# First attention: the value products of a job's four row blocks in one step

## The reference, cut to what matters

```
QEr  = einsum('bhsd,ld->bhsl', q, Er);  Srel = _skew(QEr)
QK   = einsum('bhsd,bhtd->bhst', q, k)
attn = softmax(where(causal, (QK + Srel) / sqrt(16), -inf))
out  = einsum('bhst,bhtd->bhsd', attn, v)
```

## Time and profile before

| | |
|---|---|
| median of 3 runs | 2192.8 us (2190.79 to 2193.58) |
| profiled execution | 2194.78 us |
| its span, from the first to the last instruction | 2193.1 us |
| TensorE matmul busy | 1909.3 us, 87% |
| VectorE, ScalarE, GpSimd busy | 1013.6, 854.2, 604.6 us |
| chain that ended last, by engine | PE 79%, POOL 6%, issue 5%, DVE 5%, ACT 3%, DMA 1% |
| chain, line L692 (the value products) | 2% |

### The profile page before, as it was taken

The page is one execution under the profiler, slowest core; times in us unless marked ns, Lnnn a source line. Parts: engine busy times, 40 slices in busy tenths (PEclk is TensorE's granted clock), DMA queues, the critical chain, the costliest instruction groups (busy, mean ns, idle before and its releaser), DMA issues.

```text
span 2193.1 us, 32078 instructions
## 1 busy us (share of the span) xinstructions
PE 1909.3 (87%) x10730; PEld 1108.3 (51%) x10731; DVE 1013.6 (46%) x2762; ACT 854.2 (39%) x2087; POOL 604.6 (28%) x543
## 2 busy tenths in 40 slices
PE   4899999599999963999999089999999999967998
PEld 2355555254344452666676034445445445446886
DVE  3366667634554243222222444444444444445775
ACT  2477777324444420333333044444444444421000
POOL 0011111301111115000000656665655555631000
PEclk8799999699999765999999589999999999986999
DMA  3677776300000352011100500000000000020001
GB/s 135 216 262 268 267 264 232 116 0 1 1 1 1 117 194 82 29 33 33 33 31 24 206 1 1 1 1 1 1 1 1 1 1 1 1 77 1 0 0 38
DMA packets 63567, 146.59 MB, mean 67 GB/s; under 512 B 6280, under 2 KB 41232, under 8 KB 58832
## 3 DMA queue, kind: packets, MB, share of 16 engines
q1 hardware_dynamic: 60368, 136.55, 18.1%
q0 software_dynamic: 3072, 8.39, 1.1%
HBM read 86.21 MB, written 58.72 MB: 66 GB/s over the span
## 4 chain that ended last, share of the span: by engine, by line
PE 79%; POOL 6%; issue 5%; DVE 5%; ACT 3%; DMA 1%; SPq 0%; DVEq 0%; ACTq 0%; POOLq 0%
PE PS L598 13%; PE PS L1038 8%; PE PS L889 6%; PE PS L877 6%; PE PS L967 5%; PE PS L977 5%; PE PS L990 5%; PE PS L659 4%; PE PS L746 4%; PE PS L681 3%; POOL P L581 3%; PE PS L946 3%; PE PS L955 3%; PE PS L758 2%; PE PS L692 2%
## 5 line engine op out<-in xcount | busy, mean ns | idle before, releaser
L581 POOL TENSOR_SCALAR P<-P,rc 128x512 f32<-128x512 f32 x256 | 396.8, 1562 | 266.2 <-DVE rc L1568 266.2
L1222 ACT ACTIVATE P<-PS,nm 128x512 f32<-128x512 f32 x256 | 173.5, 682 | 320.0 <-DVE nm L1562 320.0
L1562 DVE TENSOR_REDUCE nm<-PS 128x2 f32<-128x1024 f32 x128 | 156.7, 1224 | 152.9 <-PE PS L967 152.9
L977 PEld LDWEIGHTS PS<-idf,P 128*128 128x128 f32 x1024 | 110.2, 141 | 135.1 <-POOL P L581 111.6
L977 PE MATMUL PS<-idf,P 128*128 128x128 f32 x1024 | 140.7, 281 | 35.5 <-POOL P L581 35.5
L1386 DVE CUSTOM_DVE_ANT_0 dump<-PS,maskw 128x128 f32<-128x128 f32 (+3 forms) x256 | 115.6, 488 | 116.0 <-PE PS L746 114.3
L1326 DVE CUSTOM_DVE_ANT_0 SN<-PS,SR 128x128 f32<-128x128 f32 (+3 forms) x256 | 115.3, 488 | 109.2 <-PE PS L663 108.8
L1150 ACT ACTIVATE PTf<-PS 128x512 f32<-128x512 f32 (+3 forms) x256 | 101.0, 439 | 151.5 <-PE PS L758 151.4
L877 PE MATMUL PS<-EW,hT 128*128 x640 | 146.6, 383 | 2.4 <-ACT hT L1197 2.4
L889 PE MATMUL PS<-EW,xT 128*128 x320 | 146.6, 601 | 1.8 <-ACT xT L1185 1.3
L967 PE MATMUL PS<-K,Q 64*128 64x512 f32 x512 | 144.6, 641 | 0.9 <-DVE Q L1550 0.9
(11 more groups left out here) (221 smaller groups left out, 3260.5 us busy)
## 6 DMA issues: line engine op xcount, KB each, us to landing
rel<-EN SPq DMA_DIRECT2D x16, 1024.0 KB, 4.8
SR<-rel SPq DMA_DIRECT2D x16, 1024.0 KB, 7.1
rel<-EN SPq DMA_DIRECT2D x16, 768.0 KB, 4.2
SR<-rel SPq DMA_DIRECT2D x16, 768.0 KB, 6.3
rel<-EN SPq DMA_DIRECT2D x16, 512.0 KB, 2.9
SR<-rel SPq DMA_DIRECT2D x16, 512.0 KB, 4.3
EW<-in_fc1T SPq DMA_DIRECT2D x8, 1024.0 KB, 11.8
EW<-in_fc2T SPq DMA_DIRECT2D x8, 1024.0 KB, 12.3
```

The costliest lines, as they stand in the source:

```text
L581: last = nc.gpsimd.tensor_scalar(P1[s % 4][:, j, :], P1[s % 4][:, j, :], rc1[:, s % 4, j:j + 1], None, ALU.mult)
L977: last = nc.tensor.transpose(TR1[j][:, c * P:c * P + P], P1[s % 4][:, j, c * P:c * P + P], idf[:])
L1222: last = af(P1[s % 4][:, j, :], PD[s % 2][:, j, :], ACT.Exp, bias=nm1[:, s % 4, j:j + 1], accum_out=sm1[:, s % 4, j:j + 1])
```

## The change

The value products of all four row blocks of a job are issued in step 4, in the order of the row blocks; before, row block u - 3 was issued in steps 3 to 6. Nothing else is edited.

```
-                    if n >= 1 and 3 <= u < 3 + RT:
-                        values_a(n - 1, u - 3)
+                    if n >= 1 and u == 4:
+                        for r in range(RT):
+                            values_a(n - 1, r)
```

## The result

The changed kernel takes 2202.6 us (median of 6 runs, 2198.6 to 2205.2), the kernel before 2193.0 (6 runs of the same sessions, 2190.8 to 2195.5): a ratio of 1.0040, with a 95% interval of 1.0028 to 1.0052. It is slower by 9.6 us, and the forecast was 2201.3.

A forecast was written before the change was run, and what follows sets the result against it. TensorE looked the bound, but ScalarE's score copy and VectorE's output stood close behind. Terms 7.0 + 0.8 + 1.0 gave 8.8, taken as 8.5 on 2192.8: 2201.3 us, range 2198 to 2203, wider 2195.5 to 2206.

The forecast's parts named there:

- The block: Step 4: all 80 value records in one group take 2.32 us; four groups were 2.68, saving 0.36 per job.
- Step 3 for nothing: Removing step 3's 8 value records gains nothing: its scores to step 4's stay 1.41 us, waiting for ScalarE's copy.
- EN late in steps 5 and 6: Without products, ScalarE's score copy is late: 1.84 us from step 5 scores to step 6, 2.27 from step 6 to 7.
- S7 to T0, ScalarE's queue: Step 7 scores to the next job's first scores: ScalarE's queue without slack makes the latter start 0.48 us late.
- its 5.43: Time in us from step 6 scores to the transposes after the next job's first scores, read from job 0.
- the projection is 0.58 late: Next job's key projection waits for VectorE's last output: 0.58 us late per job, 7.0 over jobs 1 to 12.
- Job 13 to job 14's transposes: At the end of job 13, transposes after the next first scores wait for VectorE's copies: 0.78 us late.
- Jobs 14 and 15: Jobs without relative scores: step 6 scores come 1.03 us late, the transposes that follow 0.49 late in each job.
- The range: 0.40 to 0.65 us a job giving 5.5 to 10 in all; kernel 2198 to 2203 us, widened to 2195.5 to 2206.
- A, TensorE bounds: Faster: score copies keep up, each job gains 0.36 us and the 0.58 gap goes; 2180 us, half of it 2187; 5%.
- B, the gap takes the delay up: No change: the 0.58 us gap before the next job's first scores absorbs the delay; 2194 to 2196 us; 13%.
- C, nothing is made up: Clearly slower: none of step 4's 1.76 us is made up, late scores reaching VectorE's maxima and loads; 2216 us; 3%.

The follow-up runs named there:

- block 0 put behind: Changed kernel with row block 0's 8 value records moved from step 4 to step 5, behind its transposes: job 20.21 us, median 2202.8 us, ratio to before 1.0041.
- early output copy: Changed kernel with ScalarE's output copy moved from step 6 to step 5, ahead of its relative-score copy: job 20.43 us, median 2202.8 us, ratio to before 1.0044.
- the kernel of 19.22 us a job: Kernel before, with block 3's products ahead of step 6's transposes and one VectorE probability copy moved to ScalarE: 2188.5 us, ratio 0.9960.
- later projections: Three projections and their copies one step later: on the changed kernel 2200.0 us; on the kernel before with block 3 ahead of step 6's transposes 2197.4 us.

## Why the prediction was right

- *The block.* 2.32 us was worked out from groups of 16 and 32; it stands 2.31 from its start to the next scores (211.89 to 214.20).
- *Step 3 for nothing.* S3 to S4 is 1.41 still. Shown by the profile after and, alone, by block 0 in step 4.
- *EN late in steps 5 and 6.* 1.84 and 2.26 against 1.84 and 2.27. Shown to be lack of cover by block 0 put behind, which used the idle for nothing.
- *S7 to T0, ScalarE's queue.* 2.67, as worked out. But the early output copy shows that this wait alone does not set the time. In the changed kernel the transposes behind T0 start 5.43 us after S6 with no idle ahead of them; with T0 0.34 earlier they start at 5.43 again, now after 0.34 of idle for VectorE's copy. ScalarE and VectorE allow them at the same moment. The prediction had both engines, with its 5.43 and its 0.58.
- *The term that was mis-sized* is the last: "the projection is 0.58 late", and "I see nothing that makes up the 0.58". The projection starts 0.59 late by the rows (12.02 after S4 in place of 11.43). But from its start to S1 it took 1.91 in place of 1.82, so a job pays 0.68, which is above the prediction's own 0.40 to 0.65 a job. The longer projection goes with its wait for VectorE's output. Wherever its first weight load waits for that output (0.09 to 0.17 us), in the kernel of 19.22 us a job too, the projection takes 1.91 to 1.92. Where it does not wait it takes 1.81: in job 0 of the same traces, in all steady jobs of the kernel before, and with later projections (226.34 to 228.15). The difference stands between the first and the second of its records. The trace of the kernel before had this case once, at the end of job 13, where it could have been read:

```profile
357.08 1.98 PE L598 MATMUL PS<-CTA,WAk 128*128 128x512 f32 x4
358.99 0.49 PE L663 MATMUL PS<-Ka,QPa 32*128 32x128 f32 x4
```

  Why a projection that waited takes 0.10 longer stays open. Twelve jobs make 8.0 in place of 7.0 (S4 of job 1 to S4 of job 13: 235.19 before, 243.23 after); 12 x 0.68 is 8.2, and the 0.17 less is the one long job (19.92) in the trace of the kernel before.
- *The rest of the sum.* Job 13 to job 14's transposes: 0.76, forecast 0.78. Jobs 14 and 15: 0.30 and 0.31, forecast 0.49 each. In job 14 S6 came 1.02 late, as forecast (1.03), but the next transposes started 5.25 after S6 (374.79 to 380.04) and not the 5.43 taken from job 0. In all it is 9.42 against 8.8, of which I had taken 8.5; the medians say 9.6. So the twelve jobs cost 1.0 more than forecast and the last ones 0.4 less, and it is partly luck that the sum came this close.
- *The range.* The prediction says that 0.40 to 0.65 a job give 5.5 to 10. With its 1.8 for the last jobs they give 6.6 to 9.6. The medians' 9.6 has an interval of about 6 to 11 us, so it bears out the size of the sum, and only the rows tell its terms.
- *Rivals.* A, TensorE bounds: excluded by each experiment that merged groups and got a longer job (block 0 to step 4, block 3 to step 5). Its counter-argument that in job 0 steps without products gain at most half of them was a little off: S6 to S7 gains 0.61 of 1.00. B, the gap takes the delay up: the gap did shrink from 0.58 to 0.28, but ScalarE and VectorE kept the rest. C, nothing is made up: of the block's 1.75, 0.38 and 0.62 were won back in steps 5 and 6 and 0.29 before T0. The loads and their masks play no visible part: TensorE's waits name none, and the kernels with blocks elsewhere follow the sums without them.

The rule of the Trainium skill that rotating banks cover an evacuation (Perfetto Trace Analysis, Matmuls) agrees: the relative scores don't rotate, and the price is 0.33 us of idle in each step without products. The drain at a change of tiling mode (TensorEngine Tiling (Array Packing), Key Properties) is consistent with 0.12 us a group, but no run here separates it from other costs of a group, and it is the small term.

## What to carry to other kernels

Small products that stand between two uses of a bank that is not doubled cover the time in which the bank is emptied. Taking them away wins only what they take beyond that time. Ask of every step what it will wait for when they go, and read it from a stretch where they are missing already, as job 0 here. When a gap is removed and nothing is won, look for a second engine that holds the same place, and relieve both. And judge a change of a few microseconds by the period of the loop it touches, since start and tail of an execution drift by more.

## What the runs showed that I had not expected

TensorE's granted clock fell to 0.50 (1.2 GHz) in the last two jobs of the stage in four of the thirteen profiled executions (marked * above), though TensorE was hardly idle: in the window ahead of the fall shown above it was busy 5.64 of 6 us, with no single idle over 0.36, and during it 6.00 of 6. The kernel before has a similar share there (9.64 of 10 us from 350 to 360) and kept 1.00. The fall lasted from a few to some 20 us and cost up to 8 or 9 us: jobs of 24.35 and 17.41 where the kernel before has 17.26 and 15.51 and the changed one 17.50 and 15.81. Two executions of one program had it in different lengths, so part of the spread of the runs may be from here; only the profiled executions show their clock by stretch. What sets it off I could not settle.

Besides, the profiled executions reached job 0's S4 anywhere between 88.4 and 96.4 us, with identical code up to there on every engine in most of them, and took 1791 to 1799 us behind the stage. So a median can differ by several us from what the stage gives: block 0 behind has a stage 2.9 us shorter than the changed kernel and the same median.
